# A decoder layer on one core: cross-attention ordered by tables for the first, middle and last group of heads, and reordered feed-forward chains

## The reference

```
x = LN(x + selfattn(x))       # one head of 512; scores = triu(q k^T / sqrt(512)); a score of 0 becomes -9e15; softmax
x = LN(x + crossattn(x, ctx)) # 16 heads of 64; q = x Wq + bq, k = ctx Wk + bk, v = ctx Wv + bv; q / sqrt(8); softmax; @ Wo + bo
x = LN(x + x Ws^T + w * (x We^T) + bias)
# w: sum of the two largest of softmax(x Wg) over 7 gates, each divided by that same sum
```

## Time and profile before

| | |
|---|---|
| three runs | 2018.53, 2017.41, 2013.05 us, median 2017.41 |
| the profiled execution | 2012.89 us, its span 2011.2 us, so 1.7 us lie around the span |
| TensorE busy | 1958.3 us of the span, 97% |
| VectorE, ScalarE, GpSimd busy | 1484.3, 1163.0, 713.5 us |
| mean granted TensorE clock | 0.991 of full speed |
| where the stages lie | self-attention to about 356 us, cross-attention to about 1780 us, feed-forward to the end |

### The profile page before, as it was taken

The page is one execution under the profiler, slowest core; times in us unless marked ns, Lnnn a source line. Parts: engine busy times, 40 slices in busy tenths (PEclk is TensorE's granted clock), DMA queues, the critical chain, the costliest instruction groups (busy, mean ns, idle before and its releaser), DMA issues. The chain is left out here.

```text
span 2011.2 us, 29627 instructions
## 1 busy us (share of the span) xinstructions
PE 1958.3 (97%) x9856; PEld 1639.6 (82%) x9856; DVE 1484.3 (74%) x3162; ACT 1163.0 (58%) x2467; POOL 713.5 (35%) x839
## 2 busy tenths in 40 slices
PE   8999999799999999999999999999999999889997
PEld 7888888578888888888888888888888888667786
DVE  5767676577777777777777777777777777778886
ACT  5455544566666666666666666666666666622221
POOL 2222432132333333233333324333332333346763
PEclk9999999999999999999999999999999999989999
DMA  5778778552543525354452744535264453122121
GB/s 209 282 280 296 292 274 343 194 189 88 196 149 124 193 69 195 109 168 168 150 197 63 241 126 158 167 106 188 73 201 134 140 191 124 53 90 69 61 81 63
DMA packets 111223, 326.49 MB, mean 162 GB/s; under 512 B 9056, under 2 KB 9056, under 8 KB 107104
## 3 DMA queue, kind: packets, MB, share of 16 engines
q1 hardware_dynamic: 111072, 324.59, 47.6%
HBM read 207.12 MB, written 83.89 MB: 145 GB/s over the span
## 5 line engine op out<-in xcount | busy, mean ns | idle before, releaser
L927 POOL TENSOR_SCALAR c_prob<-c_prob,all_rden 128x512 f32<-128x512 f32 x512 | 348.6, 693 | 950.4 <-DVE all_rden L1076 950.3
L978 ACT ACTIVATE c_prob<-a_score,all_negmax 128x512 f32<-128x512 f32 x512 | 348.1, 685 | 400.4 <-DVE all_negmax L1070 400.4
L1111 DVE TENSOR_TENSOR c_pt<-a_turned,c_pt 128x512 fp32r<-128x512 f32 x512 | 330.9, 687 | 179.9 <-ACT c_pt L1005 176.0
L1070 DVE TENSOR_REDUCE all_negmax<-a_score 128x1 f32<-128x512 f32 x512 | 328.5, 681 | 6.3 <-PE a_score L1246 6.1
L1246 PE MATMUL a_score<-c_ks,c_qs 128*128 128x512 f32 x1024 | 305.3, 418 | 11.5 <-DMA c_ks<-c_ks 6.4
L1005 ACT CAST c_pt<-a_turned 128x512 fp32r<-128x512 f32 x512 | 274.8, 587 | 36.3 <-PE a_turned L1257 32.8
L1270 PE MATMUL a_av<-c_pt,c_vs 128*128 128x512 f32 x1024 | 280.0, 393 | 13.3 <-DVE c_pt L1111 13.3
L1257 PEld LDWEIGHTS a_turned<-all_ident,c_prob 128*128 128x128 f32 x2048 | 241.1, 141 | 37.1 <-POOL c_prob L927 1.3
L1257 PE MATMUL a_turned<-all_ident,c_prob 128*128 128x128 f32 x2048 | 269.6, 274 | 0.6 <-POOL c_prob L927 0.5
L1270 PEld LDWEIGHTS a_av<-c_pt,c_vs 128*128 128x128 f32 x1024 | 192.0, 189 | 56.9 <-issue 8.7
L1246 PEld LDWEIGHTS a_score<-c_ks,c_qs 128*128 128x128 f32 x1024 | 174.2, 191 | 34.7 <-issue 7.4
(11 more groups left out here) (170 smaller groups left out, 2769.9 us busy)
## 6 DMA issues: line engine op xcount, KB each, us to landing
all_first_buffer<-ctxT_scratch SPq DMA_DIRECT2D x64, 512.0 KB, 7.1
c_wk<-wk_scratch SPq DMA_DIRECT2D x64, 512.0 KB, 3.9
c_wq<-wq_scratch SPq DMA_DIRECT2D x64, 512.0 KB, 4.8
all_second_buffer<-x1T_scratch SPq DMA_DIRECT2D x16, 2048.0 KB, 11.8
c_ks<-c_ks SPq DMA_DIRECT2D x128, 256.0 KB, 3.3
ctxT_scratch<-s_csp SPq DMA_DIRECT2D x8, 2048.0 KB, 7.4
c_y<-y_steps_scratch SPq DMA_DIRECT2D x16, 1024.0 KB, 5.6
y_steps_scratch<-c_y SPq DMA_DIRECT2D x15, 1024.0 KB, 6.2
```

Of the source, the lines that this page charges most:

```text
L927: nc.gpsimd.tensor_scalar(prob[:, n % 2, i, :], prob[:, n % 2, i, :], rden[:, n % 2, i:i + 1], 1.0, ALU.mult, ALU.mult).then_inc(p_ready, 1)
L978: nc.scalar.activation(prob[:, n % 2, i, :], spsum[:, i % 2, :], ACT.Exp, bias=negmax[:, n % 2, i:i + 1], scale=1.0, accum_out=den[:, n % ...
L1070: nc.vector.tensor_reduce(negmax[:, n % 2, i:i + 1], spsum[:, i % 2, :], AX.X, ALU.max, negate=True).then_inc(smax, 1)
L1111: nc.vector.tensor_tensor(pt[:, t % 2, LO, :], tpsum[:, t % 2, :], as_f32(pt[:, t % 2, HI, :]), ALU.subtract).then_inc(pt_lo, 1)
```

## The change

The list `SLOTS` becomes three tables, from which one order of all 256 projections is made. The prologue before the first group makes V0 K0 Q0 V1 K1 Q1 (V2 moves into the first group). In a step with a projection TensorE now makes the projection first and the scores after it; `values` run four tiles late instead of two (`pt` has four slots). DVE finishes the previous step's projection ahead of the two maxima instead of after them, and in holes it takes over part of its work one step later. The outputs of heads go to a buffer with four slots (`osum`) instead of two. SP issues the copy of the first key pair ahead of the stores of self-attention's last sequence. In the last group the norm of the feed-forward's first batch is spread over steps 3 to 8. `Norm` takes 10 instructions instead of 12 with fewer waits, and in the feed-forward EXPERT comes before SHARED, the logits are turned in the middle of the first product, and the last batch is normalised tile by tile.

```diff
-    SLOTS = ["V3", "K2", "O0", "Q2", "O1", "O2", "K3", "Q3", "O3", "V0+", "K0+", "Q0+", "V1+", "V2+", "K1+", "Q1+"]
+    PROLOGUE = [("V", 0, 0), ("K", 0, 0), ("Q", 0, 0), ("V", 0, 1), ("K", 0, 1), ("Q", 0, 1)]
+    NEXT = ["V0+", "K0+", "Q0+", "V1+", "V2+", "K1+", "Q1+"]
+    MIDDLE = ["V3", "K2", "Q2", "O0", "O1", "O2", "K3", "Q3", "O3"] + NEXT
+    FIRST = ["V2", "V3", "K2", "", "Q2", "", "K3", "Q3", ""]
+    LAST = ["V3", "K2", "", "O0", "Q2", "", "O1", "K3", "Q3", "", "O2", "", "O3", "", "", ""]
     # sync_first
         sp.wait_ge(proj_mm, made("K", 0, 0))
         load_pair(wk, wkparts, 1, wk_loaded)
+        double_k(0, 0)
+        sp.wait_ge(proj_mm, made("Q", 0, 0))
+        load_pair(wq, wqparts, 1, wq_loaded)
         before.store_y(NB - 1)
-        double_k(-1, "K0+")
-        sp.wait_ge(proj_mm, made(-1, "Q0+"))
-        load_pair(wq, wqparts, 1, wq_loaded)
         before.sync_last_x1T()
...
+        before.sync_last_parts()      # the stores, before issued ahead of the wk load
     # tensor_group, a step with a projection
-                for tile in tiles:
-                    scores(*tile)
-                bank_free(g, name, first)
-                project(g, name, u)
+                project(item)
+                for tile in tiles:
+                    scores(*tile)
     # vector_group
+            left = hole(g, step - 1)
+            if not left:
+                finish(item_before(g, step))
+            if item is None:
+                if tiles:
+                    max_tile(*tiles[0])
+                if left:
+                    rest_of_hole(g, step - 1)
+                if tiles:
+                    max_tile(*tiles[1])
+                pt_lo_tile(g, 2 * step)
+                if tiles:
+                    recip(*tiles[0])
     # scalar_group: the high part of a projection ahead of the exponentials; in the last group
+            if last and step == 6:
+                held.norm2.root(nc, 0)
     # norm_first, called by vector_group in the last group
+        if step in (3, 4):
+            for i in (2 * step - 6, 2 * step - 5):
+                norm2.stats(nc, 0, i, x2)
+        if step == 6:
+            norm2.variance(nc, 0)
+        if step == 7:
+            norm2.inverse(nc, 0)
+        if step in (7, 8):
+            norm2.scale(nc, x2, x2, (2 * step - 14, 2 * step - 13))
     # tensor_all, after the last group
-        for i in range(T):
-            if i >= 2:
-                pe.wait_ge(wo_out, T * (GROUPS - 1) + i - 1)
-            project(GROUPS, f"O{i}", 0)
+        for item in EPILOGUE[:2]:
+            project(item, range(K - 1))
+        for item in EPILOGUE[:2]:
+            project(item, [K - 1])
+        for item in EPILOGUE[2:]:
+            project(item)
     # feed_forward, vector: step(b, u, c, more) with more
-                    finish_tile(b, u, 0)
-                        norm2.variance(nc, b + 1)
-                        norm2.inverse(nc, b + 1)
-                        norm2.scale(nc, x2[:, nu], x2[:, nu])
-                    finish_tile(b, u, 1)
+                    for i in (0, 1):
+                        norm2.stats(nc, b + 1, i, x2[:, nu])
+                    route_weights(b)
+                    add_expert(b, u, 0)
+                    for i in (2, 3):
+                        norm2.stats(nc, b + 1, i, x2[:, nu])
+                    norm2.variance(nc, b + 1)
+                    add_shared(b, u, 0)
+                    norm2.inverse(nc, b + 1)
+                    add_expert(b, u, 1)
+                    norm2.scale(nc, x2[:, nu], x2[:, nu])
+                    add_shared(b, u, 1)
     # feed_forward, tensor: an EXPERT product waits for add_expert two tiles before, a SHARED one for add_shared
+                    first, second = (EXPERT, SHARED) if b else (SHARED, EXPERT)
+                    product(b, u, 0, first, lambda: turn_logits(b))
```

720 lines of the change are left out of this document (373 added, 347 removed).

## The result

The changed kernel took 2002.21 us (median of 4 runs, 2001.44 to 2002.52) beside 2015.23 us for the kernel before (4 runs), ratio 0.9939, 95% interval 0.9927 to 0.9952. A second set of 5 runs, made with the experiments, gave 0.9916 (0.9903 to 0.9929). It is faster, as forecast, and inside the range 1980 to 2006; but the profiled executions differ by 2012.89 - 2001.44 = 11.4 us where my sum said 21, and the own range of that sum, 1987 to 1999, is missed by these runs (the second set's median, 1998.83, lies just inside). So the work is to find where 10 us went.

A forecast was written before the change was run, and what follows sets the result against it. TensorE, busy 1958 of 2011 us, was taken as the bound. Terms -9.1 - 5.8 + 0 + 1 - 4.2 - 2.95 = -21 us from 2012.9 gave 1992, taken as 1993; own range 1987 to 1999, with rivals 1980 to 2006.

The forecast's parts named there:

- Way in, -9.1: Before the first group: an earlier key copy ends the first scores' 6.41 us wait and slow clock; gain 9.1 us, bounds 0 and 9.1.
- First group, -5.8: First group's holes: losses fall from 10.8 to 5.0 us as a projection precedes the scores; gain 5.8, bounds 3 and 9.
- Middle groups, +1: 14 middle groups, already full: no gain possible, a loss of 1 us in all, bounds 0 and 8.
- the cover is 0.2 us: Middle groups: K2's low part, started 3.7 us late and lasting 1.5, is ready at 5.2 us; TensorE wants its bank at 5.43.
- Last group, 0: Last group and O products: losses of 18.3 us against 17.9 before, taken as 0; bounds gain 9 and loss 6.
- the count by hand: Last group, step by step: hole 2 2.2 us, hole 5 with step 6 3.6, hole 9 5.2, later steps more; sum 18.3.
- Feed-forward, -4.2: Feed-forward: TensorE's six waits of 0.7 us for the SHARED sum go; gain 4.2 us, lower bound 3.
- All three slacks: Feed-forward: DVE's spare time before the waiting EXPERT product, SHARED of tile 2 and the turn: 2.5, 2.1 and 0.6 us.
- Tail, -2.95: Behind the last product: earlier EXPERT sum, one tile scaled instead of four, four small steps fewer; gain 2.95 us.
- Values late: Values four tiles late: worth one pair of values, 0.46 us per hole, not the 13.3 us wait of values.
- Rival (b): Last group's lag worse, near 6 us lost, and middle banks cost a few us: 2001 us; chance 0.12.
- Rival (a): Scattered holes help the last group as much as the first, 8 to 9 us more gain: 1984 us; chance 0.25.

The follow-up runs named there:

- the first execution: The changed kernel as profiled first, compared with the profile of the kernel before; span 1999.7 us, median of its runs 2002.21 us, ratio 0.9939.
- the second execution: The changed kernel run again without any edit, on another chip, and profiled; 1998.83 us, ratio 0.9916 to the kernel before, span 1996.0 us.
- The experiment with K2's low part: Changed kernel with K2's low part on DVE right behind the maxima of its own step in the 14 middle groups; 1993.26 us, ratio 0.9896.
- the old table: Changed kernel with the middle groups' table in the order V3 K2 O0 Q2 O1 again, as before the change; 2053.97 us, ratio 1.0199.
- the one comparison that was run: Norm back under the O products and K2's low part early, 1987.01 us; the same with the last group's seven holes in one row, 1983.58 us.

## Why the prediction came out as it did

The direction and most mechanisms were right; the terms were mis-sized, and two of them, the middle and the last group, gave away half of the gain. That the time still fell inside the range is in part luck: in the first execution the attention's terms promised 2.5 + 4.45 + 6.6 = 13.5 us too much, and feed-forward and tail, which gave 3.1 + 0.85 = 4 us more than foreseen, covered some of it.

- **Way in, -9.1.** Time and place of the copy were right. I left out that the next scores then wait for the first exponentials (1.9 us), and that a clock can fall behind that. **First group, -5.8:** the holes lost 5.6 us against 5.0 counted. The two terms together were foreseen at 14.9 and measured 12.4 and 14.8. That the order on SP is what frees the way in is shown (7 us without it).
- **Middle groups, +1.** The step that failed is "the cover is 0.2 us ... I take a loss of 1 us in all". I had the right bank and the right 3.7 and 1.5 us. The low part ended 0.2 us late, not early, and that in all 14 groups: 5 us, inside my bounds 0 to 8. A cover of 0.2 us that is met in every group should have been taken at the middle of its bounds. The experiment with K2's low part gives all of it back.
- **Last group, 0.** The step that failed is the count by hand. By the steps of the second execution, less 5.44 us for a full step and 2.72 for a hole, hole 2 (2.7 us lost against 2.2) and hole 5 with step 6 (3.65 against 3.6) were nearly right. Hole 9 lost 7.0 and not 5.2: I put ACT's square root into its queue without its two table loads of 1.28 us, which no row of before that I used showed (its trace has one, 1.28 us at 1764.27, under the O products). Steps 10 and 11 lost 1.45 together, not 2.8. The last steps lost 6.3, not 4.5 (19.92 us for steps 12 to 15 and the last values, against 13.6 without a wait). The hand count also has no clock: behind the waits of hole 9 and of the last steps the matmuls ran slow (4 products of a turn in 1.01 to 1.11 us against 0.60), so how the excess of these two divides between the work that I left out and the clock is not shown. And of POOL's 1.6 us, "now hidden", the 18 products returned 0.4 (16.2 us from the last hole to the first turn, against 16.6). Without the norm there the term is 0 (100.6 against 100.5).
- **Feed-forward, -4.2.** All three slacks held. I took the waits from the list, six of 0.7 us; the batches are 1.22 us shorter each, since another stop of 0.28 us is on no row of TensorE, and a product with a wait of 0.71 us lasts 0.86 us longer from start to start (1879.10 to 1882.68, against 2.72). Two period lengths show it, 27.09 us before and 25.87 now, which TensorE's list of waits doesn't. **Tail, -2.95:** measured 3.8; the store behind the last scaling is 0.6 us shorter too.
- **Values late** was read rightly: worth 4 to 5 us, not the 13.3 of its wait. I did not see that it asks for O0 a step later (39 us of waits with the old table).

Rival (b) gave the time, 2001, and its two reasons, the last group near 6 us worse and a few us of banks in the middle, are what happened. I gave it 0.12, since I had counted the norm's work without its place. Rival (a) fell: scattered holes did not help, and in the one comparison that was run they are dearer than a row of them.

## What to carry to other kernels

Measure a change by landmarks, the start of the same piece of work in both timelines, and a full window by its count of instructions: 100% busy hid 5 us here, and a list of waits hid 3 more. Work that lies under something long (a norm under 18 products) gains nothing by moving ahead, and where its engine is waited for it can cost about its full time (here 5.8 to 6.5 us for 6.4 us of DVE's work), with the table loads of a function that alternates with another. If an engine stands idle in front of one operation and works late on another, change their order before the table of the whole: a low part moved on DVE gave more (5.4 us in the middle) than any of the new orders on TensorE that were tried here.

## What the hardware showed that I had not expected

- Two executions of one program differ by 3.7 us in span, 3 of them at two places with the same waits: behind a wait of 1.9 us the granted clock was 0.72 over 4 us in one and 1.00 in the other (5.49 or 3.95 us to the next scores), behind waits of 0.65 and 1.57 us a step and its hole took 12.28 or 10.83 us. The Trainium skill (TensorE: Matmul & The Clock Gate, "What's actually happening") says that the number of cold matmuls at the start of a kernel varies from run to run. These traces show the same behind short waits in the middle of one. A term for the clock behind a wait of 1 to 2 us should carry both values.
- Small DVE operations start 0.07 to 0.09 us apart without a wait between them and 0.18 to 0.20 with one. Of these three in the variance of the last tile (timeline of DVE) only the third waits for those ahead of it:

```profile
1995.05 0.16 DVE L78 TENSOR_TENSOR f_norm_t<-f_norm_stat 128x1 f32<-128x1 f32 x1
1995.12 0.15 DVE L79 SCALAR_TENSOR_TENSOR f_norm_u<-f_norm_stat 128x1 f32<-128x1 f32 x1
1995.31 0.16 DVE L82 SCALAR_TENSOR_TENSOR f_norm_t<-f_norm_t 128x1 f32<-128x1 f32 x1
```
